# One attention layer in a chain of eight: from a software loop per batch to one pipeline over 64 head pairs, with the exponentials as the stationary operand of the weighted sums

## The reference, cut to what matters

```python
x = x + _L1_xattn_ref(_layernorm(x), ctx_1024, fside, fside, Wq, Wkv, Wout, bout)

q = (x @ Wq).reshape(b, n, 32, 8)
k, v = jnp.split(ctx @ Wkv, 2, axis=-1)     # 32 heads of 8 each
q = apply_axial_rope(q, pos_map)
k = apply_axial_rope(k, ctx_pos_map)
logits = jnp.einsum('bqhd,bkhd->bhqk', q, k) * scale
w = jax.nn.softmax(logits, axis=-1)
attn = jnp.einsum('bhqk,bkhd->bqhd', w, v).reshape(b, n, 256)
return attn @ Wout + bout
```

## Time and profile before

| | us |
|---|---|
| median of 3 runs | 1949.05 |
| the profiled execution, its own time | 1958.82 |
| its span, first to last instruction | 1956.9 |
| attention pipeline, first transposes to last addition to x (385.5 to 648.4) | 262.9 |
| of it `turn(-1)` | 45.5 |
| of it three turns of the loop | 3 x 57.0 |
| of it `turn(3)` | 35.0 |
| of it output projection | 11.4 |

### The profile page before, as it was taken

How to read it: one execution, slowest core, us unless ns; L and a number is a source line. 1 busy time by engine, 2 the same in 40 slices (tenths; PEclk the granted TensorE clock), 3 DMA queues, 4 the chain that set the end, 5 groups by cost and what they waited for, 6 DMA issues and landing times.

```text
span 1956.9 us, 25669 instructions
## 1 busy us (share of the span) xinstructions
PE 1511.6 (77%) x7979; PEld 1055.7 (54%) x7979; DVE 1046.1 (53%) x2049; ACT 726.8 (37%) x1794; POOL 235.6 (12%) x343
## 2 busy tenths in 40 slices
PE   3566699548888546789897479927999999779998
PEld 1122565423333334657566369817888888565554
DVE  6899445864542694745747412233545544634444
ACT  3455111625555352523534012215556555320010
POOL 2122000200000001120211110043222222000000
PEclk7788799758988767999998689968999999979998
DMA  1000100100000001000001288610000000100000
GB/s 36 0 0 0 73 1 0 62 1 1 0 0 0 3 1 60 1 27 9 19 0 62 80 287 309 231 56 17 16 16 17 21 16 11 41 0 32 31 31 21
DMA packets 25260, 77.85 MB, mean 40 GB/s; under 512 B 3753, under 2 KB 15473, under 8 KB 21105
## 3 DMA queue, kind: packets, MB, share of 16 engines
q1 hardware_dynamic: 23664, 72.89, 10.7%
q0 software_dynamic: 1536, 4.20, 0.6%
HBM read 67.90 MB, written 9.18 MB: 39 GB/s over the span
## 4 chain that ended last, share of the span: by engine, by line
PE 61%; DVE 21%; issue 8%; ACT 6%; POOL 2%; DMA 1%; DVEq 1%; SPq 0%; ACTq 0%; POOLq 0%
PE psum L2257 4%; PE psum L1705 4%; DVE roomA L502 4%; PE psum L2266 4%; PE psum L667 3%; PE psum L1934 3%; PE psum L1405 3%; PE psum L1459 3%; PE psum L1937 3%; PE psum L2002 3%; DVE roomB L1058 3%; PE psum L1975 3%; PE psum L820 3%; PE psum L1714 2%; PE psum L1953 2%
## 5 line engine op out<-in xcount | busy, mean ns | idle before, releaser
L1058 DVE TENSOR_REDUCE roomB<-psum 128x4 f32<-128x1024 f32 x64 | 78.4, 1226 | 70.4 <-PE psum L830 70.4
L380 PE MATMUL psum<-roomA,own 128*128 128x512 f32 x128 | 75.6, 721 | 36.9 <-POOL roomA L544 36.7
L2040 ACT ACTIVATE roomA<-psum,roomA 128x256 f32<-128x256 f32 x128 | 60.3, 484 | 87.4 <-DVE roomA L2099 87.4
L2257 PE MATMUL psum<-roomA,roomB 128*128 128x512 f32 (+1 forms) x192 | 88.3, 610 | 0.0
L960 ACT ACTIVATE roomA<-psum 128x1024 f32<-128x1024 f32 x64 | 65.7, 1026 | 54.9 <-PE psum L843 54.9
L2306 ACT ACTIVATE roomA<-psum 48x512 f32<-48x512 f32 (+1 forms) x32 | 19.0, 594 | 175.1 <-PE psum L2257 175.1
L2022 ACT ACTIVATE roomA<-psum 128x128 f32<-128x128 f32 x256 | 66.7, 294 | 36.0 <-PE psum L1937 27.6
L1482 ACT ACTIVATE roomA<-psum,roomA 128x128 f32<-128x128 f32 (+1 forms) x128 | 52.7, 416 | 73.0 <-DVE roomA L1523 68.8
L1811 DVE SCALAR_TENSOR_TENSOR roomA<-roomA,psum 128x512 f32<-128x512 f32 x23 | 15.9, 689 | 119.7 <-ACT roomA L1748 119.7
L2266 PE MATMUL psum<-roomB,roomA 48*128 48x256 f32 (+1 forms) x256 | 74.9, 441 | 6.2 <-DVE roomA L2382 6.2
L1934 PE MATMUL psum<-roomB,own 128*128 128x128 f32 x512 | 65.9, 284 | 17.3 <-DVE roomA L2089 16.5
(11 more groups left out here) (409 smaller groups left out, 3590.7 us busy)
## 6 DMA issues: line engine op xcount, KB each, us to landing
roomB<-m_w_dram SPq DMA_DIRECT2D x12, 1536.0 KB, 8.4
roomA<-m_w_dram SPq DMA_DIRECT2D x11, 1536.0 KB
roomB<-f_w_dram SPq DMA_DIRECT2D x8, 752.0 KB, 4.2
roomB<-a_w_dram SPq DMA_DIRECT2D x4, 1280.0 KB, 6.1
roomB<-a_qkv_dram SPq DMA_DIRECT2D x16, 256.0 KB, 2.6
m_rows<-roomA SPq DMA_DIRECT2D x1, 2944.0 KB, 10.1
m_sums<-roomA SPq DMA_DIRECT2D x23, 128.0 KB, 8.5
roomB<-f_up_dram SPq DMA_DIRECT2D x2, 1152.0 KB, 6.6
```

The lines of the kernel that those rows point to most:

```text
L380: ins = pe.matmul(g.bank(2 * j + half), g.ident, hC[:, j, half * HALF:(half + 1) * HALF], start=False, stop=False, skip_group_check=True)
L1058: dve.tensor_reduce(maxneg[:, :, 2 * hp:2 * hp + 2].rearrange("p q m -> p m q"), scores, AX.X, ALU.max, negate=True).then_inc(s["a1_max_re ...
L2257: ins = pe.matmul(g.bank(bank, rows=m), gu[:, kt, at:at + m], xg[:, q, kt, half * HALF:(half + 1) * HALF], start=(kt == 0), stop=(kt == KD ...
```

## The change

The turns and the loop are gone. All 64 head pairs run through one unrolled pipeline of steps. Step n makes the maxima of pair n, and the scores and exponentials of pair n - 13 (`LAG`).

- `weigh(p)` covers two head pairs (four heads) and comes every second step. The exponentials are now the stationary operand, 128 by 128 floats, and 9 columns of V are moved through them: 4 heads x 2 query tiles x 2 key tiles = 16 matmuls. The sums come out with queries in rows, so the copy of L964, the transposes of L884 and the copy of V (L950) are gone. DVE divides after every fourth step (`keep`).
- `for_maxima(step, m)` is split by head: two matmuls into bank m, and DVE takes the maxima of each 512 columns by itself, so two banks alternate.
- The split maxima (`split`, every 8 steps) no longer go through `aug` and a second transpose of the queries. They are transposed alone (two small transposes, kind "M"), copied, stored to DRAM, and loaded back by DMA into three rows of the transposed queries (`a1_rows`). For each batch this replaces 4 sets of 8 transposes and 4 copies by 4 small transposes, 2 copies, 2 stores and 4 loads.
- Transposes go through banks 6 and 7 in a `ring`, one set of 8 every second step.
- `project_out(t)` is done batch by batch instead of for all four at the end; the rounding of the next layer's weights moves to steps 64 to 73.
- There are four buffers of exponentials instead of two (`slot`), and two for transposed queries and for keys.

```diff
+        def weigh(p):
+            t, quarter = p // 8, p // 2
+            pe.wait_ge(s["a1_exp"], 2 * p + 2)
+            if p % 2 == 0 and quarter >= 2:
+                pe.wait_ge(s["a1_attn"], quarter - 1)
+            for k in range(4):
+                h = 4 * (p % 8) + k
+                for qt in range(2):
+                    at = (4 + quarter % 2) * HALF + (8 * qt + h % 8) * (HD + 1)
...
-                        ins = pe.matmul(g.ps[32 * (h % 4):32 * (h % 4) + HD + 1, 4 * HALF + (h // 4) * S:4 * HALF + (h // 4 + 1) * S],
-                                        Vb[:, kt, h, :], PT[:, hp % 2, m, kt, :], start=(kt == 0), stop=(kt == 1))
...
+                        ins = pe.matmul(g.ps[:, at:at + HD + 1], slot(2 * p + k // 2)[:, k % 2, kt, qt * P:(qt + 1) * P],
+                                        V[:, 2 * t + kt, h, :], start=(kt == 0), stop=(kt == 1))
+            ins.then_inc(s["a1_pv"], 1)
```

The ring, the waits, and PE's order in a step:

```diff
+    LAG = 13
+    ring = [(-1, "T", 0, k) for k in range(4)] + [(k, "T", 0, 4 + k) for k in range(4)]
+    ring += [(16 * t - 10 + 2 * k, "T", t, k) for t in range(1, B) for k in range(8)]
+    ring += [(16 * t + 8 * hf + 9, "M", t, hf) for t in range(B) for hf in range(2)]
...
+            if step:
+                pe.wait_ge(s["a1_max_read"], 2 * step + m - 1)
...
+            if hp % 8 == 0:
+                pe.wait_ge(s[f"a1_rows{hp // 8}"], 32 * (t + 1))
+            if n:
+                pe.wait_ge(s["a1_exp"], n)
...
+            if 0 <= step - LAG < B * HP:
+                scores(step - LAG)
+            if 0 <= step < B * HP:
+                for_maxima(step, 0)
+            if pairs_at(step) is not None:
+                weigh(pairs_at(step))
+            if 0 <= step < B * HP:
+                for_maxima(step, 1)
+            while n < len(ring) and ring[n][0] == step:
+                entry(n)
+                n += 1
```

The DMAs that SP issues for the split maxima:

```diff
+                sp.wait_ge(s["a1_mt"], 2 * t + hf + 1)
+                sp.dma_start(shifts[t, hf], partsT[:, hf, :]).then_inc(s["a1_stored"], 16)
+                sp.wait_ge(s["a1_stored"], 32 * t + 16 * hf + 16)
+                for m in range(2):
+                    row = PARTS * HD + SLOT * m
+                    sp.dma_start(trQ[t % 2][row:row + 3, 8 * hf:8 * hf + 8, :],
+                                 shifts[t, hf].rearrange("(c m h) q -> c m h q", c=3, m=2)[:, m]).then_inc(s[f"a1_rows{hf}"], 16)
```

More of the change, by code:

```diff
@@ L821, in transposes @@
                 ins.then_inc(s["a1_tr_psum"], 1)
[L823 to L832, removed]
@@ L859, in turn @@
[L859 to L872, removed]
@@ L873, in turn @@
[L873 to L910, removed]
+                    ins = pe.matmul(g.bank(2 + m)[:, kt * S:(kt + 1) * S], trK[t % 2][rows, hp, kt * P:(kt + 1) * P],
+                                    trQ[t % 2][rows, hp, :], start=True, stop=True)
@@ L912, in scalar @@
+        assert n == len(ring)
     def scalar(act):
@@ L937, in scalar @@
                 act.copy(dst, src).then_inc(s["a1_dup1"], 1)
[L938 to L964, removed]
-            if A:
-                for k in range(8, 12):
-                    copies(k)
@@ new lines, in scalar @@
+        n = 0
+        for step in range(-1, STEPS):
+            e = step - LAG
+            if 0 <= e < B * HP:
+                act.wait_ge(s["a1_tsc"], e + 1)
+                if e >= 4:
+                    act.wait_ge(s["a1_pv"], (e - 4) // 2 + 1)
+                act.activation(slot(e).rearrange("p m k q -> p (m k q)"), g.ps[:, 2 * HALF:4 * HALF], ACT.Exp,
+                               scale=float(HD) ** -0.5).then_inc(s["a1_exp"], 1)
+            while n < len(ring) and ring[n][0] == step:
+                copies(n)
+                n += 1
@@ new lines, in vector @@
+        for n in range(STEPS):
+            if n and n % 8 == 0 and n <= B * HP:
+                split((n - 8) // HP, (n - 8) // 8 % 2)
+            if n < B * HP:
+                maxima(n, 0)
+                maxima(n, 1)
+            if n == 1:
+                weight_scales()
+            if quarter_at(n - 1) is not None:
+                keep(quarter_at(n - 1))
+            if n >= B * HP and (n - B * HP) % 3 == 0 and (n - B * HP) // 3 < B:
+                k = (n - B * HP) // 3
+                step(dve.tensor_tensor(g.X[:, 2 * k:2 * k + 2, :], g.X[:, 2 * k:2 * k + 2, :], bias.unsqueeze(1).to_broadcast([P, 2, D]), ALU.add))
+                round_weights(k)
+            for t in range(B):
+                if max(OUT_STEP[t] + 1, B * HP + 3 * t + 1) == n:
+                    xs = g.X[:, 2 * t:2 * t + 2, :].rearrange("p i d -> p (i d)")
+                    dve.wait_ge(s["a1_out"], t + 1)
+                    dve.tensor_tensor(xs, xs, g.bank(t % 2), ALU.add).then_inc(s["layer_done"], 1)
@@ L1104, in attn1 @@
+    base = g.done_count
     head = norm(g)
```

225 lines of the change are left out of this document (133 added, 92 removed).

## The result

| | before | after |
|---|---|---|
| median of the runs shown (4 each) | 1950.53 | 2063.94 |
| ratio, 95% interval | | 1.0583, 1.0557 to 1.0609 |
| the profiled execution's span | 1956.9 | 2063.8 |
| attention pipeline, first transposes to last addition to x | 262.9 | 375.5 |
| granted clock in it | 0.83 | 0.51 |

The change makes the kernel slower by 113.4 us, 5.8%. The direction was predicted, the size was not: 2019 was forecast, and the result lies 4 us above the top of the range, 2060. The difference is in the pipeline: 375.5 - 262.9 = 112.6. The two spans differ by less, 106.9, because outside the layer, where the code is the same, the profiled execution of the kernel before took 1694.0 us and that of the kernel after 1688.3. Over the profiles of this document this rest goes from 1677.0 to 1694.0 us, so a few us in a whole time need not be the layer's.

What follows compares the result with a forecast made beforehand. It took PE's weight loads, priced by the clock, to bound the layer: pairs 284, projection 16.5 and ends 32 made 333 us against 262.9, +70, so 2019 us in all; range 1980 to 2060, own range 1990 to 2035.

Steps and rivals of the forecast that it cites:

- The price of a `weigh`: Weighted sums of two head pairs, 32 records: 3.5 us at full clock, 7.0 at half.
- The DMA path of the maxima: Copy, store and load of the split maxima: 5.0 us, inside the 6.0 available for the first batch, so cost 0.
- The rival at full clock: Attention layer at full clock throughout, as PE never idles from step 13: layer 221 us, whole 1907; chance 0.10.
- I take one pair in six at full speed: Pairs of steps: clock mostly half, 305 x 5/6 + 180/6 = 284 us.
- rival 2: Attention layer at half clock throughout: 305 + 18 + 32 = 355 us, whole 2041; chance 0.20.
- The lead: Before the first `weigh`: weight reductions, 13 steps, a split, first transposes and some set waits, 27 us.
- The pairs, 305 and 18 for the projection: At half clock, 20 pairs of 10.1 us, 5 of 9.2 and 7 of 8.1 make 305; projection 18.
- The "+8" in the range: Allowance in the range's upper end: scores and maxima apart could take 0.6 instead of 0.54 us, +8.
- The end, 5: After the last `weigh`: a division, transposes, a copy, four matmuls and an addition, 5 us.
- Loads that keep their pace (4): Weight loads of `weigh` keep full-clock pace at half clock: layer 243 us, whole 1929; chance 0.03.
- loads that hide (5): Weight loads vanish behind other matmuls, so DVE bounds: layer 151 us, whole 1837; chance 0.02.
- a late DMA path (6): Maxima's DMA at 10.1 us each way takes 21, adding up to 29: whole 2048; chance 0.03.

Runs made afterwards that it cites:

- e_wide_last: Changed kernel with 126 columns moved per load and the weighted sums issued behind both halves of the maxima; 1922.44 us, 0.9870 of the kernel before.
- e_vstat: Changed kernel without the operand swap: V stationary, 256 columns moved, sums copied and transposed back, two exponential buffers; 1869.26 us, 0.9575 of the kernel before.
- e_few: Changed kernel with the weighted sums of three of four heads left out, so a quarter of the loads; 1898.78 us, 0.9721 of the kernel before.
- e_bf16: Changed kernel with exponentials and V held in bf16 instead of float, 16 records a `weigh` instead of 32; 1864.63 us, 0.9556 of the kernel before.
- e_last: Changed kernel with the weighted sums issued behind both halves of the maxima instead of between them; 2042.88 us, 1.0463 of the kernel before.
- e_wide: Changed kernel with the 9 columns moved fourteen times over, 126 per load, loads unchanged; 1932.12 us, 0.9883 of the kernel before.
- e_kick: Changed kernel with 126 columns moved per load in the first four pairs of steps only, 9 after; 2042.00 us, 1.0449 of the kernel before.
- e_wide7: Changed kernel with the 9 columns moved seven times over, 63 per load; 2059.66 us, 1.0546 of the kernel before.

## Why the prediction was off

**Right.** The bound: PE, with DVE and ACT waiting for it. The price of a `weigh`: 3.5 and 7.0 us forecast, 3.7 and 6.9 measured, so both levels cost what the earlier trace rows say. The rule on loads in the Trainium skill, TensorE: Matmul & The Clock Gate, section LDWEIGHTS, knows no clock; by it both would be an estimated 3.4, and the 6.9 at half clock speaks against it. The DMA path of the maxima: the first scores start at 416.14, right behind the transposes ahead of them, and no wait for `a1_rows` appears in the middle. The rival at full clock was worked out as 221 us for the layer, 1907 in all; the nearest run, `e_wide_last` (full clock, the halves together, 126 columns moved), has 236 and 1922.

**The step that failed: "I take one pair in six at full speed".** I reasoned that scores, maxima and transposes, 3.1 us of them between two `weigh`, were like the loop that held 1.00, and would lift the clock now and then. It rose once in 375 us, for the 6.8 from 702.3 on, behind the float matmuls of the projection, and not behind scores, maxima and transposes. With half clock throughout my sum is 355 instead of 333: 22 of the 42.5 us that were missing. What the loop had at 1.00 and the new pipeline has not is L855, the 256-column float matmuls among scores and maxima. `e_vstat` puts them back into the same pipeline, with the float transposes that belong to them, and has 0.99 in its middle. The earlier trace rows had the hint, since maxima alone stayed at 0.50 for 26 us. I used it for rival 2, at 0.20, where it should have led. `e_few` and `e_bf16` show it without a long run of float loads: 0.50 in both, up to the projection. What the chip counts in such a stretch stays open.

**The other 20.5 us are terms of the sum that were too small.**
- The lead, "27 us": 34.4. I counted 13 steps. There are 15 before the first `weigh`, and with the first exponential comes the load of its table, 1.28 us, while PE stands at the next scores:

```profile
417.28 1.28 ACT L998 ACT_TABLE_LOAD   x1
...
419.65 0.61 PE L892 MATMUL psum<-roomA,roomB 51*128 51x256 bf16 x4 [2.48 <-ACT roomA L998]
```

- The pairs, 305 and 18 for the projection: 333.9 together, 11 more. A pair with transposes has 10.78, not 10.1, and there are 20 of them: 14 us. My sum had no wait in it, but PE stands 0.35 us for DVE's reduction; that is the wait for `a1_max_read` that the prediction names as a sign of being wrong. And a half of the maxima issued alone takes 0.54, as long as all four matmuls together. The "+8" in the range allowed 0.06 for each group of four; the order was worth 21 us in `e_last`. A pair without maxima has 9.2 (713.23 to 722.43), not 8.1, since the second scores wait for an exponential there too: seven of them, 8 us. Against it stand the one `weigh` at 3.74 and the projection: its matmuls and transposes are busy 11.9 and 4.4 us, 16.3 and not 18, and 4.8 of these lie in the end, so that my sum counted them twice.
- The end, 5: 7.2, at half clock.

**The range.** It reached to rival 2 plus 19 us. Rival 2, half clock throughout, had the clock right but for 6.8 us, and missed the layer by 20.5, by these terms.

**The other rivals.** Full clock (3) fell, and its reason with it: PE is busy 98% of 207.5 us at 0.50 (422.50:630.00), and in `e_wide` 90% at 0.99. Its price was somewhat low: 5.7 us a pair of steps, where `e_kick`, with 126 columns moved, has 6.37 at full clock (`weigh` at 434.57 and at 440.94). By the Trainium skill, TensorE: Matmul & The Clock Gate, Part 1, a TensorE with no idle gaps is warm. The row 422.50:630.00 speaks against reading it like that. Loads that keep their pace (4) fall by the 6.92 us of a `weigh`, loads that hide (5) by the same, a late DMA path (6) by the absent wait.

## What to carry to other kernels

Before a matmul's operands are swapped, price both sides: the columns moved became 9 instead of 256, but 16 float loads of 128 columns took their place, and the large moved operand had been what came with the full clock. If a stretch has a TensorE without idle time and a granted clock of 0.50, idle time is not what to look for; here moving the same columns fourteen times over brought the clock to 0.99 and seven times over left it at 0.50. And issue matmuls that lie in different rows of the array next to each other: a TensorE that was 98% busy still gave back 0.32 of 2.39 us a step.

## What was not expected of the hardware

- The same loads in the same order ran at a clock of 0.50 in the middle of `e_wide7` and of 0.99 in that of `e_wide`, with layers of 371.5 and 244.3 us. What tells the two apart for the chip, beyond what they move, no run here shows.
- More moved columns cost almost nothing behind these float loads: at 0.50, 63 columns take 7.09 us for 32 records, 9 take 6.99; at 0.99, 126 columns take 3.84, 9 take 3.74.
- A load and 9-column matmul takes 0.033 us in bf16 and 0.43 in float, both at the lower clock.
- Four 48-row matmuls in two row groups hold PE for 0.57 us and two in one group for 0.54, at the lower clock; 0.31 and 0.32 at the higher.
